# Row-by-row fetching by SP and ACT in the second layer's edge sweep, and PSUM operands on VectorE beside GpSimd's gathers, in a four-layer graph network

## The chip, the cores and the metric

The kernel runs on one core of one Trainium2 chip. The metric is the device time of one execution in microseconds (us); three executions of the kernel before are shown. Engine names: PE (TensorE), DVE (VectorE), ACT (ScalarE), POOL (GpSimd), SP (SyncE). PSUM is the accumulator memory with 8 banks of 2 KB in each of 128 partitions, SBUF the working memory.

## What is computed

A graph of 12,500 nodes and 200,000 edges, sorted by destination, goes through four layers. Each adds its output to the node state x; x is normalised before each.

```python
x = x + L0(h, ...)      # attention, 1 head, batch norm, relu
x = x + L1(h, ...)      # attention, 4 heads, with 13 edge features in the logit
x = x + L2(h, ...)      # sum of 128 edge attributes per node, then a 3-layer MLP
x = x + L3(h, ...)      # one weight matrix per edge type (8), mean over a node's edges
# attention, layers L0 and L1:
alpha = leaky_relu(a_src[src] + a_dst[dst] (+ a_edge))
out   = segment_sum(softmax_over_dst(alpha) * h[src], dst) + bias
# L3:
msg = einsum('nd,rdo->rno', x, W_rel)[edge_type, src]
out = relu(x @ W_self.T + b + segment_sum(msg, dst) / deg)
```

## The kernel before

**Layout.** Nodes are padded to 128 x 98 (partition p holds nodes 98p to 98p+97, in NK = 14 chunks of JB = 7 columns). Edges are padded to 128 x EC = 1568, and each partition's 1568 edges form GK = 8 strands of 196. A sweep over the edges takes NG = 98 groups of GC = 16 columns; a group is 2 steps of all 8 strands. Because the edges are sorted by destination, a sweep is a running sum along each strand that a factor 0 cuts where the destination changes; the table `keep` holds 1 or 0 per edge.

**Stages**, one after the other, all five engines meeting in `finish_stage` (L171) between them:

1. graph: edge borders, counts, node tables, the table of layer A (L0).
2. expansion and edge sweep of layer A (also sums the 128 edge attributes).
3. node stage A (`nodes_a_stage`): softmax division, batch norm, table of layer B.
4. expansion and edge sweep of layer B (L1).
5. node stage B (`nodes_b_stage`): L1's end, the MLP L2, the relation table for L3.
6. sweep over the relation table (`edges_rel_stage`, "rel").
7. last node stage (`nodes_rel_stage`).

**A sweep.** POOL issues one indirect DMA per column: 128 rows of the node table, one for each partition, picked by an index column in SBUF (`src` for layers A and B at L1077, `rel_row` for rel at L2036). A group's rows lie in one of NS = 6 slots (5 in layer A). POOL may start on group g when the store of group g-6 has landed and group g-5 is summed. DVE then makes the logits (L1213 to L1233), ACT the exponentials (L1134) and, in layer B, a copy of the edge terms (L1136); DVE multiplies the rows (L1246) and adds the running sums (L1190, L1195, two of each per group; one operand is in PSUM). SP stores the group (L1111, in rel L2052), 1120 KB in layer B.

**Help in the rel sweep.** For every second group from 7 to 95 (45 groups, the list `HELPED`) POOL issues 15 gathers rather than 16. The rows of the last column are fetched by plain one-row DMAs whose source row comes from a register: `fetch_rows` (L1988) loads 32 indices from `helped_row` into registers (L1991), then for each one fixes the address (L1993) and issues one DMA (L1994). SP does 32 rows after each group's store, ACT 32 rows after each group's L2069, so that two group times give the 128 rows. The table `helped_row` is `rel_row`'s columns turned by PE: it is made at the start of node stage B (DVE L1872, L1874, PE L1942, DVE L1878). PE's program there first waits for all seven weight loads of ACT's queue (L1763).

**Expansion** (`Expand`). The destination logits lie at the first edge of each node and are spread along the edges by a scan, one per head (L715), whose two inputs are `keep` and the logits, both in SBUF. In layer B the edge terms are then added to all heads (L755), and a scan per head sums the edge terms themselves (L759). POOL meanwhile gathers the first groups of the sweep.

**Node stages.** POOL gathers seven columns of the sums per chunk (L1280). In stage A `AttentionNodes.v_join` multiplies both parts by their factors (L1373, L1375) and adds them (L1377), 896 elements per partition each, all operands in SBUF; the next bias is added at L1512. The sums have two buffers: chunk k+2 is gathered once chunk k is joined. In the last stage each chunk takes three such operations (L2154, L2156, L2158), with three buffers.

## Time and profile before

| | us |
|---|---|
| runs | 7205.66, 7193.89, 7196.95 (median 7196.95) |
| profiled execution | 7196.47, of which span 7194.6 |
| POOL busy | 5087.8 (71% of the span), 5295 instructions |
| DVE busy | 3425.5 (48%) |
| ACT busy | 985.2 (14%) |
| PE busy | 624.0 (9%) |

A busy time counts an engine's own instructions; DMA issues and register loads on SP and ACT are not in it. POOL's time is that of the indirect DMAs it issues. A "mean ns" is the duration of one; POOL also spends some 300 ns between two of them, shown as idle time released by "issue".

### The profile page before, as it was taken

The numbers are of one execution on the slowest core, as the hardware profiler recorded it, in microseconds if no ns is written. First come the engines' busy times: TensorE is split into PE (matmuls) and PEld (weight loads), VectorE is DVE, ScalarE is ACT, GpSimd is POOL, SyncE is SP. The second block draws the span as 40 slices with busy tenths as digits, with TensorE's granted clock in tenths as the row PEclk, the third lists the DMA queues.
The fourth block names the chain that finished last, engine by engine and source line by source line (L and its number), as shares of the span: only waits on it lengthen the run. The fifth ranks groups of instructions, "written<-read, shape, count | busy, mean of one in ns | idle before, by whom it ended". The sixth has DMA issues, their size and how long they took to land. (4 is left out here: it accounts for less than half of the span.)

```text
span 7194.6 us, 39656 instructions
## 1 busy us (share of the span) xinstructions
PE 624.0 (9%) x2403; PEld 426.9 (6%) x2403; DVE 3425.5 (48%) x6202; ACT 985.2 (14%) x3082; POOL 5087.8 (71%) x5295
## 2 busy tenths in 40 slices
PE   1100000000001530000000000058411000000000
PEld 1100000000000420000000000024200000000000
DVE  8466666666666664444444444478322222222223
ACT  2122222222222120000000000056200000000000
POOL 5777777777775577777777777633477777777776
PEclk7555555555555665555555555579755555555555
DMA  5366767676765423333333333345333333333332
GB/s 182 111 213 210 224 210 225 209 226 209 225 209 180 147 98 113 115 115 115 115 115 115 115 115 115 101 160 201 139 107 108 113 108 107 110 110 107 107 112 86
DMA packets 334692, 1044.18 MB, mean 145 GB/s; under 512 B 106489, under 2 KB 128764, under 8 KB 296514
## 3 DMA queue, kind: packets, MB, share of 16 engines
q1 hardware_dynamic: 151986, 668.92, 25.9%
q0 software_dynamic: 173632, 368.42, 20.3%
q10 hardware_dynamic: 8784, 4.31, 0.2%
q14 instruction: 271, 2.22, 0.1%
q8 instruction: 19, 0.31, 0.0%
HBM read 527.27 MB, written 513.96 MB: 145 GB/s over the span
## 5 line engine op out<-in xcount | busy, mean ns | idle before, releaser
L1077 POOL DMA_INDIRECT edge_rows<-table_b,src_i x1568 | 1502.2, 958 | 477.8 <-issue 477.8
L1077 POOL DMA_INDIRECT edge_rows<-table_a,src_i x1568 | 1483.9, 946 | 477.9 <-issue 477.9
L2036 POOL DMA_INDIRECT edge_rows<-table_rel,rel_row x1523 | 1437.0, 944 | 510.3 <-issue 462.8
L2121 DVE TENSOR_TENSOR edge_rows<-edge_rows,ps 128x1024 f32<-128x1024 f32 x195 | 238.0, 1221 | 1386.9 <-DMA edge_rows<-table_rel,rel_row 1383.5
L1213 DVE TENSOR_TENSOR z<-edge_rows,dst_logit 128x16 f32<-128x16 f32 (+1 forms) x196 | 40.9, 209 | 1679.1 <-DMA edge_rows<-table_b,src_i 1026.4
L1195 DVE TENSOR_TENSOR edge_rows<-edge_rows,ps 128x1032 f32<-128x1032 f32 (+1 forms) x390 | 484.2, 1242 | 84.4 <-ACT edge_rows L1131 67.3
L1190 DVE TENSOR_TENSOR ps<-edge_rows,ps 128x1032 f32<-128x1032 f32 (+1 forms) x390 | 485.7, 1245 | 8.6 <-ACT edge_rows L1131 1.9
L1131 ACT ACTIVATE edge_rows<-edge_rows,weight_decay 128x129 f32<-128x129 f32 x1568 | 470.1, 389 | 0.0
L805 PE MATMUL ps<-ident,edge_rows 128*128 128x128 f32 x16 | 3.9, 426 | 3483.2 <-DVE edge_rows L1195 2034.1
L1134 ACT ACTIVATE ps<-weight_decay 128x128 f32<-128x128 f32 x98 | 27.5, 281 | 1893.4 <-DVE weight_decay L1233 1893.4
L2069 ACT ACTIVATE ps<-keep 128x16 f32<-128x16 f32 x98 | 19.6, 201 | 1850.7 <-DVE edge_rows L2121 1847.0
L2107 DVE TENSOR_TENSOR ps<-edge_rows,ps 128x1024 f32<-128x1024 f32 x195 | 239.5, 1228 | 35.9 <-DMA edge_rows<-table_rel,rel_row 29.2
L1246 DVE TENSOR_TENSOR edge_rows<-edge_rows,ps 128x2112 f32<-128x2112 f32 x98 | 230.7, 2354 | 35.3 <-ACT ps L1134 35.3
L1165 DVE TENSOR_TENSOR ps<-edge_rows,ps 128x1024 f32<-128x1024 f32 x195 | 239.5, 1228 | 0.0
L1173 DVE TENSOR_TENSOR edge_rows<-edge_rows,ps 128x1024 f32<-128x1024 f32 x195 | 236.7, 1214 | 0.1
L1127 ACT ACTIVATE weight_decay<-weight_decay 128x16 f32<-128x16 f32 x98 | 21.2, 216 | 1472.1 <-DVE weight_decay L1233 1472.1
L805 PEld LDWEIGHTS ps<-ident,edge_rows 128*128 128x128 f32 x16 | 3.1, 223 | 3483.8 <-issue 2034.4
L1934 PE MATMUL ps<-w_rel,own_part 128*128 128x512 f32 x392 | 196.7, 641 | 2.5 <-DVE rel L1838 1.2
L912 PE MATMUL ps<-ident,edge_rows 128*1 128x128 f32 (+1 forms) x16 | 3.8, 416 | 2037.5 <-DVE edge_rows L1195 2037.5
L1280 POOL DMA_INDIRECT node_sums<-sums_b,sum_row x98 | 102.5, 1046 | 93.5 <-DVE out_b L1377 52.1
L1751 POOL TENSOR_TENSOR x<-x,par 128x896 f32<-128x896 f32 x14 | 29.2, 2084 | 185.2 <-ACT hn L1645 185.2
L510 POOL DMA_INDIRECT piece<-dst_float,q_i x99 | 98.3, 993 | 79.3 <-DVE q_i L532 50.6
(284 smaller groups left out, 3211.9 us busy)
## 6 DMA issues: line engine op xcount, KB each, us to landing
sums_a<-edge_rows SPq DMA_DIRECT2D x98, 2064.0 KB, 8.2
sums_b<-edge_rows SPq DMA_DIRECT2D x98, 1120.0 KB, 4.7
edge_rows<-in_ea SPq DMA_DIRECT2D x98, 1024.0 KB, 11.8
sums_rel<-edge_rows SPq DMA_DIRECT2D x98, 1024.0 KB, 4.1
table_rel<-rel SPq DMA_DIRECT2D x98, 512.0 KB, 3.0
edge_rows<-table_rel ACTq DMA_DIRECT2D x2880, 0.5 KB
edge_rows<-table_rel SPq DMA_DIRECT2D x2880, 0.5 KB
edge_rows<-table_a,src_i POOLq DMA_INDIRECT x1568
```

Source lines behind the costliest of these rows:

```text
L1077: e.indirect_dma_start(out=rows[:, s, i, 0:L.W], out_offset=None, in_=L.table, in_offset=bass.IndirectOffsetOnAxis(ap=src[:, at:at + 1], a ...
L1131: done = e.activation(R[:, i, 0:NW], R[:, i, 0:NW], ACT.Copy, scale=wd[:, g % 2, 0, i, :])
L1165: attr_step.append(then(e.tensor_tensor(old_attr, before(g, t)[:, :, L.W:L.WS], bc(keep_now[:, t, :].unsqueeze(2), [P, GK, D]), ALU.mult)))
L1173: done = e.tensor_tensor(now, now, old_attr, ALU.add)
L1190: done = then(e.tensor_tensor(heads(old), heads(before(g, t)), bc(decay_now.unsqueeze(3), [P, GK, H, C + 1]), ALU.mult))
L1195: done = e.tensor_tensor(now, now, old, ALU.add)
L1246: t_weight = then(e.tensor_tensor(heads(R), heads(R), bc(factors[:, 0, :, :].unsqueeze(3), [P, GC, H, C + 1]), ALU.mult))
L1280: e.indirect_dma_start(out=self.buf[:, k % self.depth, b, :], out_offset=None, in_=self.sums, in_offset=bass.IndirectOffsetOnAxis(ap=sum_r ...
L1934: done = e.matmul(ps[:, 4 + 2 * (j % 2) + h, 0:half * D], own_part[:, j, :], w_rel[:, h * half:(h + 1) * half, :].rearrange("p r d -> p (r ...
L2036: e.indirect_dma_start(out=rows[:, s, i, :], out_offset=None, in_=table_rel, in_offset=bass.IndirectOffsetOnAxis(ap=rel_row[:, at:at + 1], ...
L2107: e.tensor_tensor(old, before, keep_now, ALU.mult).then_inc(step.sem, 1)
L2121: i = e.tensor_tensor(steps(g)[:, t, :, :], steps(g)[:, t, :, :], old, ALU.add)
```

## The change

It has three parts.

1. **Row-by-row fetching in layer B's sweep.** A class `Helped` takes the place of `fetch_rows` and serves both sweeps. In layer B (not in A) POOL drops the last column of the 45 groups 7, 9, ..., 95; SP and ACT fetch those rows, 140 elements each, in quarters of 32: SP quarter 0 of group g+4 and quarter 1 of g+3 after storing group g, ACT quarter 2 of g+3 and quarter 3 of g+2 after the exponentials and the copy of group g. Each of these calls waits first for the store of the group six before, and for the sum of the group five before, the one it is to fill. In the rel sweep the order stays as it was. Three semaphores take the place of four.
2. **The index tables** `helped_src` and `helped_rel` are both made in the graph stage (a memset, two copies, two transposes, two copies out of PSUM), and the four instructions at the start of node stage B go.
3. **PSUM operands.** ACT copies `keep` to PSUM (`near`) at the start of both expansions, and the scans read it there. In layer B the scan of a head writes to PSUM and the edge terms are added head by head, in place of one add over all heads. In node stage A the factors and the first product are in PSUM; in the last stage the inverse degrees and the mean are.

The core of the diff:

```diff
+    class Helped:
+        def fetch(self, e, regs, g, p0, n):
+
+            if g not in self.place:
+                return
+            h, s = self.place[g], g % self.NS
+            e.wait_ge(*self.stored[s].at(16 * (g // self.NS)))
+            e.wait_ge(*self.summed.at(g - self.NS + 2))
+            for p in range(p0, p0 + n, len(regs)):
+                m = min(len(regs), p0 + n - p)
+                e.load(regs[0:m], self.index[h:h + 1, p:p + m])
+                for i in range(m):
+                    row = e.snap(regs[i])
+                    e.dma_start(self.rows[p + i:p + i + 1, s, LAST, 0:self.W], self.table[bass.ds(row, 1), :]
+                                ).then_inc(self.fetched[h % 3].sem, 16)
...
-        def v_spread(self, e):
+        def s_near(self, e):
+            e.activation(self.near, keep[:, :], ACT.Copy).then_inc(self.keep_near.sem, 1)
+
+        def v_spread(self, e, terms=None):
...
             for h in range(self.L.H):
-                e.tensor_tensor_scan(self.dst_l[:, :, h], keep[:, :], self.dst_l[:, :, h], 0.0, ALU.mult, ALU.add
+                at = self.dst_l[:, :, h]
+                e.tensor_tensor_scan(at if terms is None else self.spread, self.near, at, 0.0, ALU.mult, ALU.add
                                      ).then_inc(step.sem, 1)
                 step.up()
+                e.wait_ge(*step.at(step.n))
+                if terms is not None:
+                    e.tensor_tensor(at, terms[:, :, h], self.spread, ALU.add).then_inc(step.sem, 1)
...
-                for i in range(GC):
+                for i in range(GC - (g in helped.place)):
...
+                if L.AE:
+                    helped.fetch(e, regs_sync, g + 4, 0, P // 4)
+                    helped.fetch(e, regs_sync, g + 3, P // 4, P // 4)
...
+                    helped.fetch(e, regs_scalar, g + 3, P // 2, P // 4)
+                    helped.fetch(e, regs_scalar, g + 2, 3 * P // 4, P // 4)
...
-            then(e.tensor_tensor(a[:, :, :, 0:C], a[:, :, :, 0:C], bc(of_sums.unsqueeze(3), wide), ALU.mult))
+            then(e.tensor_tensor(part, a[:, :, :, 0:C], bc(by_sums.unsqueeze(3), wide), ALU.mult))
...
-            t = then(e.tensor_tensor(b[:, :, :, 0:C], b[:, :, :, 0:C], bc(of_own.unsqueeze(3), wide), ALU.mult))
-            e.wait_ge(*step.at(t))
-            e.tensor_tensor(out, a[:, :, :, 0:C], b[:, :, :, 0:C], ALU.add).then_inc(self.joined.sem, 1)
+            t = then(e.tensor_tensor(b[:, :, :, 0:C], b[:, :, :, 0:C], bc(by_own.unsqueeze(3), wide), ALU.mult))
+            e.wait_ge(*step.at(t))
+            e.tensor_tensor(out, b[:, :, :, 0:C], part, ALU.add).then_inc(self.joined.sem, 1)
...
-            nodes.v_logit(e, 0, step)
-            e.wait_ge(*helped_turned.at(1))
-            then(e.tensor_copy(helped_row[:, :], ps[:, 1, 0:P]))
+            nodes.v_logit(e, 0, step)
...
-                t = then(e.tensor_tensor(r, r, bc(inv_deg[:, span(k)].unsqueeze(2), [P, JB, D]), ALU.mult))
+                if k >= 1:
+                    e.wait_ge(*out_ready.at(k))
+                t = then(e.tensor_tensor(mean, r, bc(inv_near[:, span(k)].unsqueeze(2), [P, JB, D]), ALU.mult))
                 e.wait_ge(*step.at(t))
-                t = then(e.tensor_tensor(r, r, chunk(own_part, k), ALU.add))
+                t = then(e.tensor_tensor(mean, chunk(own_part, k), mean, ALU.add))
                 e.wait_ge(*step.at(t))
-                e.scalar_tensor_tensor(r, r, 0.0, chunk(x, k), ALU.max, ALU.add).then_inc(out_ready.sem, 1)
+                e.scalar_tensor_tensor(r, mean, 0.0, chunk(x, k), ALU.max, ALU.add).then_inc(out_ready.sem, 1)
```

**What stands in a row on the engines.** ACT in layer B's sweep, with the change, at the first helped group (`weight_decay` are the log weights, `helped_src` the index table, `ISA` fixes an address in a register; the pair ISA and DMA stands 32 times):

```order
L1211 ACTIVATE ps<-weight_decay 128x128 [waits edges_for_exp]
L1213 ACTIVATE edge_rows<-edge_logit 128x16x4
L240 TENSOR_LOAD helped_src [waits edges_summed,edges_stored1]
L242 ISA
L243 DMA edge_rows<-table_b 1x140
L242 ISA
L243 DMA edge_rows<-table_b 1x140
```

Before, ACT's two activations of a group were followed at once by those of the next group; now a load and 32 row DMAs stand between them.

DVE in layer B's expansion, before (a scan is printed as SCALAR_TENSOR_TENSOR):

```order
L711 COPY dst_logit<-first_logit 128x4
L715 SCALAR_TENSOR_TENSOR dst_logit<-keep,dst_logit 128x1568 x4
L752 MEMSET keep 128x8
L755 TENSOR_TENSOR dst_logit<-dst_logit,edge_logit 128x6272
L759 SCALAR_TENSOR_TENSOR edge_logit<-keep,edge_logit 128x1568 x4
```

and with the change:

```order
L774 COPY dst_logit<-first_logit 128x4
L780 SCALAR_TENSOR_TENSOR ps<-ps,dst_logit 128x1568
L785 TENSOR_TENSOR dst_logit<-edge_logit,ps 128x1568
L780 SCALAR_TENSOR_TENSOR ps<-ps,dst_logit 128x1568
L785 TENSOR_TENSOR dst_logit<-edge_logit,ps 128x1568
L780 SCALAR_TENSOR_TENSOR ps<-ps,dst_logit 128x1568
L785 TENSOR_TENSOR dst_logit<-edge_logit,ps 128x1568
L780 SCALAR_TENSOR_TENSOR ps<-ps,dst_logit 128x1568
L785 TENSOR_TENSOR dst_logit<-edge_logit,ps 128x1568
L827 MEMSET keep 128x8
L827 MEMSET ps 128x8
L831 SCALAR_TENSOR_TENSOR edge_logit<-ps,edge_logit 128x1568 x4
```

Each of the large operations now has one input in PSUM and one in SBUF; the add is cut in four and stands between the scans.

DVE at the start of node stage B, before (L1325 to L1338 make the first chunk's logits, L1361 begins its join):

```order
L1872 MEMSET helped_f 128x128
L1874 CAST helped_f<-rel_row 128x45
L1325 TENSOR_TENSOR self_logit<-own_rows,node_logit_b 128x28
...
L1338 TENSOR_TENSOR self_ex<-self_logit,self_max 128x28
L1878 CAST helped_row<-ps 128x128
L1361 TENSOR_TENSOR den<-node_sums,self_ex 128x28
```

and with the change:

```order
L1406 TENSOR_TENSOR self_logit<-own_rows,node_logit_b 128x28
L1409 TENSOR_TENSOR self_max<-node_sums,inv_deg 128x28
...
L1418 TENSOR_TENSOR self_ex<-node_sums,self_max 128x28
L1419 TENSOR_TENSOR self_ex<-self_logit,self_max 128x28
L1450 TENSOR_TENSOR den<-node_sums,self_ex 128x28
```

The copy out of PSUM between the logits and the join is gone, and with it DVE's wait for PE there.

## Rows read from the trace of the kernel before

**Rows 1.** Groups of instructions by line, POOL alone: busy us, mean ns | idle us, releasers

```profile
L1077 POOL DMA_INDIRECT edge_rows<-table_b,src_i x1568 | 1502.2, 958 | 477.8 <-issue 477.8
L1077 POOL DMA_INDIRECT edge_rows<-table_a,src_i x1568 | 1483.9, 946 | 477.9 <-issue 477.9
L2036 POOL DMA_INDIRECT edge_rows<-table_rel,rel_row x1523 | 1437.0, 944 | 510.3 <-issue 462.8 <-SPq L171 45.7 <-DVE edge_rows L2121 1.8
L1280 POOL DMA_INDIRECT node_sums<-sums_a,sum_row x98 | 110.0, 1122 | 57.2 <-issue 28.3 <-SPq L171 17.6 <-DVE agg L1377 7.4
L1280 POOL DMA_INDIRECT node_sums<-sums_rel,sum_row x98 | 104.0, 1061 | 37.4 <-issue 29.6 <-POOLq L171 7.8
```

**Rows 2.** One line's instructions: duration ns min/median/max, first and last start us

```profile
L1077 POOL DMA_INDIRECT edge_rows<-table_b,src_i x1568: 940/944/6627, 2660.9 to 4639.7; - x196
L2036 POOL DMA_INDIRECT edge_rows<-table_rel,rel_row x1523: 940/944/963, 5122.9 to 7023.6; - x191
L1280 POOL DMA_INDIRECT node_sums<-sums_rel,sum_row x98: 940/944/1859, 7052.8 to 7185.4; - x98
```

**Rows 3.** Groups by line and form, DVE, both from layer B's sweep

```profile
L1190 DVE TENSOR_TENSOR ps<-edge_rows,ps 128x1056 f32<-128x1056 f32 x195 | 245.4, 1259 | 3.4
L1213 DVE TENSOR_TENSOR z<-edge_rows,dst_logit 128x64 f32<-128x64 f32 x98 | 22.2, 227 | 1026.4 <-DMA edge_rows<-table_b,src_i 1026.4
```

**Rows 4.** Timeline of layer B's expansion: start us, duration us, instruction

```profile
2669.95 13.38 DVE L715 TENSOR_TENSOR_SCAN dst_logit<-keep,dst_logit 128x1568 f32<-128x1568 f32 x4
...
2683.50 6.69 DVE L755 TENSOR_TENSOR dst_logit<-dst_logit,edge_logit 128x6272 f32<-128x6272 f32 x1
2684.38 6.63 POOL L1077 DMA_INDIRECT edge_rows<-table_b,src_i  x1 [0.30 <-issue]
2690.22 13.38 DVE L759 TENSOR_TENSOR_SCAN edge_logit<-keep,edge_logit 128x1568 f32<-128x1568 f32 x4
...
2704.65 0.94 POOL L1077 DMA_INDIRECT edge_rows<-table_b,src_i  x1 [0.30 <-issue]
```

**Rows 5.** Timeline of layer A's expansion

```profile
326.25 3.42 DVE L715 TENSOR_TENSOR_SCAN dst_logit<-keep,dst_logit 128x1568 f32<-128x1568 f32 x1
326.60 3.83 POOL L1077 DMA_INDIRECT edge_rows<-table_a,src_i  x1 [0.30 <-issue]
```

**Rows 6.** Timeline of the rel sweep, SP and ACT: one turn of 32 rows each

```profile
5887.31 0.40 SPq L2052 DMA_DIRECT2D sums_rel<-edge_rows  x1
5892.17 13.48 SPq L1994 DMA_DIRECT2D edge_rows<-table_rel  x32
...
5887.32 0.20 ACT L2069 ACTIVATE ps<-keep 128x16 f32<-128x16 f32 x1 [19.64 <-DVE edge_rows L2121]
5891.78 13.08 ACTq L1994 DMA_DIRECT2D edge_rows<-table_rel  x32
```

**Rows 7.** Timeline of layer B's sweep, ACT: one group's two activations

```profile
3405.58 0.28 ACT L1134 ACTIVATE ps<-weight_decay 128x128 f32<-128x128 f32 x1 [19.55 <-DVE weight_decay L1233]
3405.80 0.24 ACT L1136 ACTIVATE edge_rows<-edge_logit 128x64 f32<-128x64 f32 x1
```

**Rows 8.** Timeline of node stage A, POOL: three gathers in a row, one chunk

```profile
2477.46 1.21 POOL L1280 DMA_INDIRECT node_sums<-sums_a,sum_row  x1 [0.30 <-issue]
2478.97 1.54 POOL L1280 DMA_INDIRECT node_sums<-sums_a,sum_row  x1 [0.30 <-issue]
2480.81 1.82 POOL L1280 DMA_INDIRECT node_sums<-sums_a,sum_row  x1 [0.30 <-issue]
```

**Rows 9.** Timeline of the last node stage: the stretched gather of one chunk

```profile
7171.11 1.84 POOL L1280 DMA_INDIRECT node_sums<-sums_rel,sum_row  x1 [0.30 <-issue]
```

**Rows 10.** Timeline of the start of node stage B

```profile
4696.84 0.25 ACT L1343 ACTIVATE self_ex<-self_ex 128x56 f32<-128x56 f32 x1 [20.34 <-DVE self_ex L1338]
...
4700.47 0.29 DVE L1878 CAST helped_row<-ps 128x128 int32<-128x128 f32 x1 [3.65 <-PE ps L1942]
4700.67 0.19 DVE L1361 TENSOR_TENSOR den<-node_sums,self_ex 128x28 f32<-128x28 f32 x1
```

More of the change, by code:

```diff
@@ L202, in natural, with every, helped_columns, __init__ @@
         return i % GK * NC + g * GS + i // GK
-    HELP_EVERY = 2
-    HELPED = list(range(7, NG - 1, HELP_EVERY))
+    LAST = GC - 1
+    def every(n, first):
+        return {g: h for h, g in enumerate(range(first, NG - 1, n))}
+    def helped_columns(ap, place):
+        at = [natural(g, LAST) for g in place]
+        return ap[:, at[0]:at[-1] + 1:at[1] - at[0]]
+    helped_b = every(2, 7)
+    class Helped:
+        def __init__(self, name, place, index, table, W, rows, NS, stored, summed):
+            self.place, self.index, self.table, self.W = place, index, table, W
+            self.rows, self.NS, self.stored, self.summed = rows, NS, stored, summed
+            self.by_pool = {g: 16 * sum(GC - (i in place) for i in range(g % NS, g + 1, NS)) for g in range(NG)}
+            self.fetched = [sem(f"{name}_helped{i}") for i in range(3)] if place else []
+        def all_by_pool(self, slot):
+            return self.by_pool[max(g for g in range(NG) if g % self.NS == slot)]
+        def fetch(self, e, regs, g, p0, n):
[11 more added lines that the diff above has]
+                                ).then_inc(self.fetched[h % 3].sem, 16)
+        def wait(self, e, g):
+            if g in self.place:
+                h = self.place[g]
+                e.wait_ge(*self.fetched[h % 3].at(16 * P * (h // 3 + 1)))
     def sum_rows(sums, g):
@@ L683, in tensor @@
                     table.t_turn(e, i)
+            e.wait_ge(*helped_floated.at(2))
+            for i in range(2):
+                done = e.transpose(ps[:, 7, i * P:(i + 1) * P], helped_f[:, i, :], ident[:, :])
+            done.then_inc(helped_turned.sem, 1)
         return Programs(sync, scalar, gpsimd, vector, tensor)
@@ L1028, in attention_edges @@
         factors = ps[:, 7, 0:2 * GC * H].rearrange("p (i c h) -> p i c h", i=2, c=GC)
-        gathered = [sem_of(f"edges_gathered{i}", 16 * GC * turns(NG, NS, i)) for i in range(NS)]
         stored = [sem_of(f"edges_stored{i}", 16 * turns(NG, NS, i)) for i in range(NS)]
@@ L1033, in attention_edges @@
         summed = sem_of("edges_summed", NG)
+        helped = Helped(L.name, helped_b if L.AE else {}, helped_src, L.table, L.W, rows, NS, stored, summed)
+        gathered = [sem_of(f"edges_gathered{i}", helped.all_by_pool(i)) for i in range(NS)]
         def spare(i):
@@ L1358, in v_join @@
             of_sums, of_own = self.ex[:, s, 0, :, :], self.ex[:, s, 1, :, :]
+            if self.near is None:
+                by_sums, by_own, part = of_sums, of_own, a[:, :, :, 0:C]
+            else:
+                if k >= 1:
+                    e.wait_ge(*self.joined.at(k))
+                factors, part = self.near
+                by_sums, by_own = [factors[:, i * JB * H:(i + 1) * JB * H].rearrange("p (j h) -> p j h", h=H)
+                                   for i in range(2)]
             out = self.out_of(k).rearrange("p j (h c) -> p j h c", h=H)
@@ L1987, in nodes_b_stage @@
         return Programs(sync, scalar, gpsimd, vector, tensor)
-    def fetch_rows(e, regs, table, out, of, h, p0, n, fetched):
-        e.load(regs[0:n], helped_row[h:h + 1, p0:p0 + n])
-        for m in range(n):
-            row = e.snap(regs[m])
-            e.dma_start(out[p0 + m:p0 + m + 1, of, GC - 1, :], table[bass.ds(row, 1), :]).then_inc(fetched.sem, 16)
     def edges_rel_stage(local, own_part):
@@ L2019, in edges_rel_stage @@
         summed = sem_of("edges_summed", NG)
+        helped = Helped("rel", helped_b, helped_rel, table_rel, D, rows, NS, stored, summed)
+        gathered = [sem_of(f"edges_gathered{i}", helped.all_by_pool(i)) for i in range(NS)]
         crossing = Crossing("cross", rows[:, (NG - 1) % NS, GC - GK:GC, :], sb("border_state", [P, NV + 1])[:, :],
@@ L2033, in gpsimd @@
                     e.wait_ge(*summed.at(g - NS + 2))
-                for i in range(GC - (g in place)):
+                for i in range(GC - (g in helped.place)):
                     at = natural(g, i)
@@ L2199, in _ @@
         def _(e):
+            regs_sync.extend(e.alloc_register(f"row_sync{i}") for i in range(32))
             graph.sync(e)
@@ L2217, in _ @@
         def _(e):
+            regs_scalar.extend(e.alloc_register(f"row_scalar{i}") for i in range(32))
             graph.scalar(e)
```

103 lines of the change are left out of this document (54 added, 49 removed).

## The prediction

> **What bounds the kernel now.** I read three views, in this order. First the groups of instructions of POOL [rows 1]: the two attention sweeps are 1568 gathers each and the rel sweep 1523, every one about 945 ns busy with some 305 ns of "issue" behind it. In all three the idle time is issue and next to nothing else: POOL never waits for a free slot, so it sets the pace. Then one line's instructions with first and last start [rows 2]: in layer B 1568 gathers go from 2660.9 to 4639.7 us; in rel 1523 go from 5122.9 to 7023.6, a pitch of 1900.7 / 1522 = 1.249 us. Last DVE [rows 3]: in layer B it sat idle 1026 us for gathered rows, 10.5 us a group. What shortens POOL's row of gathers shortens these stages one for one; what DVE or ACT do there costs nothing until it exceeds a group's time of 16 x 1.249 = 20.0 us.
>
> **Why some gathers are long.** In layer B's expansion the timeline [rows 4] shows a gather of 6.63 us that starts during the add of 6.69 us (L755) and ends 0.8 us after it. Both inputs of that add are in SBUF. Under the scans, which also have both inputs there, the gathers take some 3.0 to 3.3 us: from 2660.9 [rows 2] to 2704.65 [rows 4] POOL starts 17 gathers, 43.8 us, where its own pitch would need far less. Layer A's one scan stretches one gather to 3.83 us [rows 5]. In the sweeps DVE runs operations of 1.26 us with one operand in PSUM, 195 of the shown form alone [rows 3], and POOL's median stays at 944 ns [rows 2]. So a long DVE operation with two SBUF inputs holds a gather back, and one with a PSUM operand does not. I take that as the mechanism.
>
> Against it stands the Trainium skill, page "SBUF — State Buffer", section "Who interferes with whom", which tells of a probe in which `tensor_tensor` did not stall a GpSimd DMA, and infers that descriptor generation does not need the interface that the second input takes. By that rule part 3 of the change would be worth nothing. The same section also has two SBUF inputs contend with a GpSimd instruction that reads SBUF; the gathers of this kernel take their indices from SBUF, and the 6.63 us row sides with this second statement.
>
> **The change, part by part.**
>
> *Layer B's sweep.* POOL issues 45 gathers less. Its pitch there after the expansion is (4639.7 - 2704.65) / 1550 = 1.2484 us [rows 2, 4], and 45 x 1.2484 = **56.2 us**. That is a gain only if SP and ACT keep up. A pair of groups now takes POOL 31 gathers, 38.7 us, 19.35 us a group; the shorter group takes 18.7. SP's turn in the rel sweep runs from 5887.31 to 5892.17 + 13.48 = 5905.65, 18.3 us, of which 4.5 us are the register load and the hops around it and 13.5 the 32 DMAs [rows 6]. ACT's turn there is 5887.32 to 5904.86, 17.5 us. In layer B ACT gives up an activation of 0.20 us and has two that end 0.46 us after their start [rows 7]: 17.8 us. So SP has 1.0 us to spare per group and ACT 1.5, and DVE, which now also waits for ACT's exponentials with a row turn queued ahead of them, has its 10 us. SP's store of a group now has a row turn of the group before ahead of it, as in rel already. The row is 560 bytes rather than 512. No row shows what that does to an issue; one bound is nothing, the other proportion to bytes, 9.4% of 13.5 us or 1.3 us, with which SP would take 19.6 us, 0.3 us over the pace, 91 x 0.3 = 27 us of loss. I take nothing, since a store of 1024 KB takes SP 0.40 us to issue, no more than a row of 512 bytes with its address work, 13.48 / 32 = 0.42 us [rows 6]: issuing does not go by bytes.
>
> *Layer B's expansion.* 17 gathers at their own pitch need 21.2 us in place of 43.8: **22.6 us**. All nine disturbed ones lie under operations that now have a PSUM input. DVE's own chain stays about as long (eight scans, the add in four parts) and ends near 2704; POOL has six slots, 120 us of gathers, so nothing waits for it. ACT's copy of `keep` runs while DVE waits for the logits. The bounds are 0 (a scan that reads PSUM still blocks) and 22.6.
>
> *Layer A's expansion.* One gather goes from 3.83 to 0.94 us [rows 5]: **2.9 us**. Bounds 0 and 2.9.
>
> *Node stage A.* The 98 gathers are 110.0 us busy at a mean of 1122 ns [rows 1]; at 944 ns they would take 92.5, so 17.5 us are stretch. Three gathers of a chunk show it [rows 8]: 1.21 under the bias add, which stays as it is, 1.54 and 1.82 under the three operations of the join, which change. Per chunk that is 0.6 + 0.9 = 1.5 us, some 20 us if all 14 chunks had it; the total allows 17.5 less 14 x 0.27 for the bias, 13.7. The sums have two buffers, and POOL already waited 7.4 us for joins [rows 1]; a faster POOL will wait more, a few times. I take **12 us**, with bounds of 4 and 20.
>
> *Last node stage.* POOL gathers back to back. 13 chunks have one gather like the 1.84 us one [rows 9]; busy time 104.0 less 98 x 0.944 leaves **11.4 us**. All three operations change, and there are three buffers, so nothing takes its place: each chunk is then 8.7 us of gathers against 3.3 us of DVE. Bounds 8 and 11.5.
>
> *Start of node stage B.* ACT's exponentials end at 4697.09; DVE begins the join at 4700.67, since it waits for PE's transpose, which is behind the weight loads [rows 10]. Without the copy it can begin at some 4697.2: **3.5 us**. The stage is a chain of DVE, ACT and PE that starts there. Bounds 0 (the matrices are needed a step later anyway) and 3.5.
>
> *Graph stage.* The new table work is a handful of operations like the 0.29 us copy [rows 10], below 2 us of DVE. I cost it at nothing; DVE there ends long before POOL's last scatter. If that cover were gone it would cost these 2 us.
>
> Sum: 56.2 + 22.6 + 2.9 + 12 + 11.4 + 3.5 = 108.6. The profiled execution is 7196.5, which gives 7087.9; the median of the runs is 0.5 above it, so **7088 us**, 1.5% faster. A measurement of this kernel tells about 0.2% (14 us) from no change.
>
> **Rivals.**
>
> *A: the PSUM operands free nothing.* By the page's first statement above the sum is 56.2 + 3.5 = 59.7, 7137 us. The rows against it are the 6.63 and 3.83 us gathers. For it: no row shows a scan with a PSUM input beside a gather. 4%.
>
> *B: the row turns do not fit.* SP or ACT is a little slower per row in layer B than in rel, and the sweep goes at their pace for 91 groups. At 19.6 us for SP (the bytes bound) the time is 7088 + 27 = 7115. For it speaks how little room there is, 1.0 us of 18.3; against it that rel runs with the same turns at its own pitch, DVE waiting for gathers alone. 8%.
>
> *C: slower than before.* The same mechanism taken further: ACT stands in every group's chain, since DVE cannot weight the rows before ACT's exponentials, and ACT now issues 32 DMAs between two of them. Should the DMA queue push back (the stores are 1120 KB, in rel 1024), ACT's turn grows. The sweep gains nothing from a turn of 20.0 us on, 69 ns a row more than in rel; to eat the other 52 us as well it takes 0.57 us more for each of 91 groups, a turn of 20.6, or 495 ns a row in place of 409 [rows 6]. At 21.5 us it would be 7196 + 91 x 1.5 - 52 = 7281. In rel nothing like it is seen. 5%, of which 2 stop near the point of balance.
>
> *D: node stage A gives all or more.* If POOL's waits there shrink with the stretch, 20 us rather than 12: 7080. 12%; and if new waits take it back, 4 rather than 12: 7096. 13%.
>
> **How the numbers follow.** The forecast as it stands 58%, A 4%, B 8%, C 5%, D 25% with both signs. The range takes the forecast, both sides of D and half of B: 7070 to 7108. Slower by over 0.2% is most of C, 0.03; within 0.2% the rest of C, 0.02; all else is faster, 0.95.
>
> **What the profile after would show.** Layer B's sweep has 1523 gathers, issue as the only idle time, and no gather above 1 us in the expansion though the scans run. SP's and ACT's turns are as long as in rel, and DVE waits for POOL's rows, not for the helped ones. In the last stage every gather is 0.94 us; in node stage A one of 1.2 to 1.5 us per chunk is left. DVE starts node stage B's first join right behind the exponentials. The forecast is wrong if DVE's wait in layer B is on one-row DMAs or on ACT, if POOL there shows a wait for DVE or a store, or if gathers stay stretched under a scan that reads PSUM.

## The result and the profile after

The changed kernel takes 7092.65 us (median of 7098.0, 7091.91, 7089.11 and 7093.38) against 7196.95 before: a ratio of 0.9854, 95% interval 0.9837 to 0.9871, so 1.5% faster. The profiled execution is the longest of the four, 7098.0 us with a span of 7095.8.

POOL's groups, busy us, mean ns | idle us with what ended it, answer to [rows 1]:

```profile
L1151 POOL DMA_INDIRECT edge_rows<-table_a,src_i x1568 | 1482.6, 946 | 477.8 <-issue 477.8
L1151 POOL DMA_INDIRECT edge_rows<-table_b,src_i x1523 | 1439.0, 945 | 464.5 <-issue 464.5
L2099 POOL DMA_INDIRECT edge_rows<-table_rel,rel_row x1523 | 1438.8, 945 | 509.9 <-issue 463.7 <-SPq L173 45.7 <-DVE edge_rows L2181 0.6
...
L1360 POOL DMA_INDIRECT node_sums<-sums_a,sum_row x98 | 96.5, 984 | 63.2 <-issue 27.4 <-SPq L173 19.2 <-DVE agg L1466 12.6
...
L1360 POOL DMA_INDIRECT node_sums<-sums_rel,sum_row x98 | 92.6, 945 | 37.4 <-issue 29.6 <-POOLq L173 7.8
```

In layer B's sweep POOL issues 45 gathers less, and its only idle time is still issue (its own time between two gathers): the row turns of SP and ACT fit (a turn is what SP or ACT does for one group: a register load and 32 one-row DMAs). DVE waits there 944.5 us for POOL's gathers and not once for a one-row DMA. The mean went from 958 to 945 ns, so the long gathers of the expansion are gone as well. The last stage is back at the plain duration. Node stage A kept 4 us of stretch (96.5 against 98 x 0.945) and waits 12.6 us for DVE's join in place of 7.4.

One line's instructions, with min/median/max and first and last start, answer to [rows 2]:

```profile
L1151 POOL DMA_INDIRECT edge_rows<-table_b,src_i x1523: 940/945/966, 2651.4 to 4553.6; - x191
```

The longest of the 1523 is 966 ns; before it was 6627. Taken from such first and last starts, the stages moved like this:

| POOL's gathers | before, us | after, us | difference | predicted |
|---|---|---|---|---|
| layer A's sweep | 1960.5 | 1959.2 | -1.3 | -2.9 |
| node stage A | 147.8 | 139.5 | -8.3 | -12 |
| layer B's sweep, expansion included | 1978.8 | 1902.2 | -76.6 | -78.8 |
| from node stage B's first gather to rel's | 440.6 | 437.6 | -3.0 | -3.5 |
| rel sweep | 1900.7 | 1902.0 | +1.3 | 0 |
| last node stage | 132.6 | 121.2 | -11.4 | -11.4 |

The rows add up to -99.3 and the gaps between them to +0.5: -98.8, which is the difference of the two spans, 7194.6 and 7095.8. The profiled execution after is the longest of its four, so the medians differ by more, 104.3.

The timeline of layer B's expansion (start us, duration us, instruction) answers to [rows 4]:

```profile
2680.05 3.43 DVE L780 TENSOR_TENSOR_SCAN ps<-ps,dst_logit 128x1568 f32<-128x1568 f32 x1
2680.19 0.94 POOL L1151 DMA_INDIRECT edge_rows<-table_b,src_i  x1 [0.30 <-issue]
...
2683.52 3.01 DVE L785 TENSOR_TENSOR dst_logit<-edge_logit,ps 128x1568 f32<-128x1568 f32 x1
2683.94 0.95 POOL L1151 DMA_INDIRECT edge_rows<-table_b,src_i  x1 [0.30 <-issue]
```

Gathers that start inside a scan or an add now take 0.94 and 0.95 us. SP's and ACT's turns in layer B's sweep answer to [rows 6, 7]:

```profile
3112.33 0.40 SPq L1185 DMA_DIRECT2D sums_b<-edge_rows  x1
3117.32 13.26 SPq L243 DMA_DIRECT2D edge_rows<-table_b  x32
3131.06 0.40 SPq L1185 DMA_DIRECT2D sums_b<-edge_rows  x1
```

```profile
3104.58 0.28 ACT L1211 ACTIVATE ps<-weight_decay 128x128 f32<-128x128 f32 x1 [19.66 <-DVE weight_decay L1313]
3104.80 0.24 ACT L1213 ACTIVATE edge_rows<-edge_logit 128x64 f32<-128x64 f32 x1
3106.96 14.08 ACTq L243 DMA_DIRECT2D edge_rows<-table_b  x32
```

SP's turn is 3130.58 - 3112.33 = 18.25 us and ACT's 3121.04 - 3104.58 = 16.5. ACT's rows are a little slower than in rel (440 ns in place of 409), but its register load takes 2.15 us there against 4.08.

### The profile page after: what moved, and what is told of

It is laid out like the page before. It is cut to its first block and busy times, and to the rows that moved or that the text cites. A ratio compares the mean times of both kernels' runs of the same rounds, so it can differ in the third digit from the quotient of the medians.

```text
span 7095.8 us, 57426 instructions
## 1 busy us (share of the span) xinstructions
PE 615.7 (9%) x2404; PEld 417.4 (6%) x2404; DVE 3430.4 (48%) x6209; ACT 988.0 (14%) x3084; POOL 5001.1 (70%) x5250
## 5 line engine op out<-in xcount | busy, mean ns | idle before, releaser
L1151 POOL DMA_INDIRECT edge_rows<-table_b,src_i x1523 | 1439.0, 945 | 464.5 <-issue 464.5
L1293 DVE TENSOR_TENSOR z<-edge_rows,dst_logit 128x16 f32<-128x16 f32 (+1 forms) x196 | 40.6, 207 | 1594.7 <-DMA edge_rows<-table_b,src_i 944.5
```

The lines of the kernel that those rows point to most:

```text
L1151: e.indirect_dma_start(out=rows[:, s, i, 0:L.W], out_offset=None, in_=L.table, in_offset=bass.IndirectOffsetOnAxis(ap=src[:, at:at + 1], a ...
```

## The experiments

Unless a text says otherwise, each changes the changed kernel, and the ratio is to the kernel before in the same session (a session is one set of executions on one chip). Where a text gives microseconds above the changed kernel, they are above its 7092.65, taken in a session in which the kernel before took 7196.95; in the two sessions of the first eight experiments it took 7198.46 and 7198.08, so such a difference is good to some 3 us.

**The row turns alone undone.**

```diff
-        helped = Helped(L.name, helped_b if L.AE else {}, helped_src, L.table, L.W, rows, NS, stored, summed)
+        helped = Helped(L.name, {}, helped_src, L.table, L.W, rows, NS, stored, summed)
```

> The changed kernel without SP's and ACT's row turns in layer B's sweep; POOL gathers all 1568 there again, all PSUM operands stay. Theory (POOL's row of gathers is the whole gain of the turns): 45 x 1.2498 = 56 us longer than the changed kernel, all of it in layer B's sweep, which then takes 1902 + 56 = 1958 us; total 7149, against 7093 with the turns and 7197 before. Rival (the turns cost something beside the gain, in ACT's place in the chain or in the queue of stores): the difference is below 50 us, and the other stages change too.

Measured: 7148.9 us, ratio 0.9932 (0.9915 to 0.9948), 56.3 us above the changed kernel. The groups have 1568 gathers of layer B at the plain mean:

```profile
L1151 POOL DMA_INDIRECT edge_rows<-table_b,src_i x1568 | 1479.7, 944 | 477.8 <-issue 477.8
```

Its gathers start over 1956.2 us, where other runs with 1523 of them at 944 ns take 1900.6: 55.6 us, against 56.2 predicted. No other stage moved by more than the spread of the gathers' own pitch. The turns cost nothing where they stand.

**The PSUM operands alone undone.** Scans, adds, join and last stage as before; both sweeps keep their turns.

```diff
-                e.tensor_tensor_scan(at if terms is None else self.spread, self.near, at, 0.0, ALU.mult, ALU.add
+                e.tensor_tensor_scan(at if terms is None else self.spread, keep[:, :], at, 0.0, ALU.mult, ALU.add
...
-                t = then(e.tensor_tensor(mean, r, bc(inv_near[:, span(k)].unsqueeze(2), [P, JB, D]), ALU.mult))
+                t = then(e.tensor_tensor(r, r, bc(inv_deg[:, span(k)].unsqueeze(2), [P, JB, D]), ALU.mult))
```

> The changed kernel with the row turns in both sweeps but without the PSUM operands: the spreading of logits in both layers, the join of node stage A and the last node stage read and write SBUF as before. Theory (a DVE operation with two SBUF inputs holds a gather back, one with a PSUM input does not): longer than the changed kernel by 20.4 (layer B's expansion) + 2.9 (layer A's) + 8.3 (node stage A) + 11.4 (last stage) = 43 us, total 7136; the four stages get their times of before back. Rival (these stages became shorter because of the turns or by chance): no difference, 7093.

Measured: 7137.15 us, ratio 0.9913 (0.9897 to 0.993), 44.5 above the changed kernel, 43 expected. By first and last gather: layer B 1923.9 us, node stage A 146.8, last stage 131.6. The parts of the change add up: 56.3 + 44.5, and 3.0 for the start of node stage B, which neither run undoes, are 103.8 against the 104.3 between the medians of before and after. By the ratios the two are 56.1 and 42.5, together with the 3.0 101.6: the parts add up within some 3 us, and the closer match is luck.

**One half of layer B's expansion undone.** The first four scans read `keep` from PSUM but write SBUF; the add and the last four scans have two SBUF inputs.

```diff
-            expand.v_spread(e, edge_logit)
+            expand.v_spread(e)
...
+            e.tensor_tensor(dst_l[:, :, :], dst_l[:, :, :], edge_logit[:, :, :], ALU.add).then_inc(step.sem, 1)
...
-                e.tensor_tensor_scan(edge_logit[:, :, h], expand.near, edge_logit[:, :, h], 0.0, ALU.mult, ALU.add
+                e.tensor_tensor_scan(edge_logit[:, :, h], keep[:, :], edge_logit[:, :, h], 0.0, ALU.mult, ALU.add
```

> The changed kernel, only layer B's expansion altered: the four scans that spread the logits still read keep from PSUM (but write SBUF), while the add is one operation with two SBUF inputs again and the four scans of the edge terms read keep from SBUF. Theory (it goes operation by operation): the gathers beside the first four scans stay at 0.95 us; one beside the add is some 6.6 us, four beside the last scans some 3.1 us each, together 5.7 + 4 x 2.2 = 14 us of stretch; total 7107. Rival (it is the sum of the traffic, or where the result is written, that counts): the gathers beside the first scans are long as well, which write SBUF again, and the total is 7113.

Measured: 7108.48 us, ratio 0.9874 (0.9857 to 0.989), 15.8 above the changed kernel. Its timeline tells the operations apart:

```profile
2659.14 13.80 DVE L780 TENSOR_TENSOR_SCAN dst_logit<-ps,dst_logit 128x1568 f32<-128x1568 f32 x4
2660.09 0.94 POOL L1154 DMA_INDIRECT edge_rows<-table_b,src_i  x1 [0.31 <-issue]
...
2673.18 6.69 DVE L830 TENSOR_TENSOR dst_logit<-dst_logit,edge_logit 128x6272 f32<-128x6272 f32 x1
2673.82 6.87 POOL L1154 DMA_INDIRECT edge_rows<-table_b,src_i  x1 [0.30 <-issue]
2679.91 13.38 DVE L834 TENSOR_TENSOR_SCAN edge_logit<-keep,edge_logit 128x1568 f32<-128x1568 f32 x4
2680.99 3.09 POOL L1154 DMA_INDIRECT edge_rows<-table_b,src_i  x1 [0.31 <-issue]
```

All eleven gathers beside the first scans took 0.94 or 0.95 us although the scans write SBUF; one beside the add took 6.87 and four beside the last scans 3.0 to 3.1. In the profile before, the first four scans stood in the same place and took 13.38 us in place of 13.80 [rows 4]. Four gathers beside them took 3.0 to 3.3, the first of them

```profile
2670.88 3.25 POOL L1077 DMA_INDIRECT edge_rows<-table_b,src_i  x1 [0.30 <-issue]
```

The same operation holds a gather or doesn't, by one input.

**Does a result in PSUM do the same?** Two runs in the last stage, each with one operation that has both inputs in SBUF and writes PSUM. First the first operation of a chunk:

```diff
-                t = then(e.tensor_tensor(mean, r, bc(inv_near[:, span(k)].unsqueeze(2), [P, JB, D]), ALU.mult))
+                t = then(e.tensor_tensor(mean, r, bc(inv_deg[:, span(k)].unsqueeze(2), [P, JB, D]), ALU.mult))
```

> The changed kernel, in the last node stage only the first operation of each chunk altered: it reads the inverse degrees from SBUF again, so both its inputs are in SBUF, and writes its result to PSUM as before. Theory (what holds a gather is two inputs in SBUF): one gather of most chunks is stretched by up to that operation's 1.1 us; the 98 gathers take 3 to 9 us more than 92.6 and the stage 124 to 130 in place of 121.2; total 7095 to 7101. Rival (a result in PSUM is enough to keep the gathers free): 121.2 and 7092.

Measured: the stage took 121.1 us, all gathers 940 to 947 ns. That reads like the rival, but it isn't evidence: in 13 of the 14 chunks a gather had started up to 0.27 us ahead of that operation or within 0.02 us of its start, and the next one came behind its end or in its last 0.12 us. None started in its midst, so none could be held. The profile before agrees, in the same stage: gathers that started up to 0.03 us behind an operation weren't held, those at 0.05 to 0.10 took 1.81 to 1.86 us. (The run's total, 9763 us, belongs to a session of which more below.) So the second operation was altered instead, the one which a gather follows by 0.1 us:

```diff
-                t = then(e.tensor_tensor(mean, r, bc(inv_near[:, span(k)].unsqueeze(2), [P, JB, D]), ALU.mult))
+                t = then(e.tensor_tensor(r, r, bc(inv_near[:, span(k)].unsqueeze(2), [P, JB, D]), ALU.mult))
...
-                t = then(e.tensor_tensor(mean, chunk(own_part, k), mean, ALU.add))
+                t = then(e.tensor_tensor(mean, chunk(own_part, k), r, ALU.add))
```

> The changed kernel, in the last node stage the second operation of each chunk altered: it reads own_part and the sums, both in SBUF, and writes PSUM; the first reads its factors from PSUM and writes SBUF, the third has one PSUM input. The run that altered the first operation could not tell: no gather started between its begin and its end. The second operation is the one that a gather starts some 0.1 us behind, before the change and after. Theory (two inputs in SBUF hold a gather, wherever the result goes): that gather takes 1.82 us in about 11 of 14 chunks, the stage 11 x 0.88 = 10 us more than 121.2. Rival (the result in PSUM is enough): all gathers stay at 0.94 to 0.95 us and the stage at 121.2. Read from the stage, since the difference is near what the totals can tell.

Measured: 7115.68 us, ratio 0.9871 (0.9854 to 0.9887); the stage took 130.8 us, 9.6 more than 121.2. One chunk in its timeline:

```profile
7004.34 1.09 DVE L2220 TENSOR_TENSOR node_sums<-node_sums,ps 128x896 f32<-128x896 f32 x1 [6.17 <-DMA node_sums<-sums_rel,sum_row]
7004.41 0.94 POOL L1360 DMA_INDIRECT node_sums<-sums_rel,sum_row  x1 [0.30 <-issue]
7005.46 1.10 DVE L2222 TENSOR_TENSOR ps<-own_part,node_sums 128x896 f32<-128x896 f32 x1
7005.65 1.72 POOL L1360 DMA_INDIRECT node_sums<-sums_rel,sum_row  x1 [0.30 <-issue]
```

The gather behind L2220 (a PSUM input, result to SBUF) takes 0.94 us, the one behind L2222 (two SBUF inputs, result to PSUM) 1.72. Twelve chunks have such a gather of 1.72 to 1.80, and the five that start 0.05 to 0.07 us behind L2220 all take 0.94. It is the inputs, not where the result goes.

The Trainium skill, page "SBUF — State Buffer", section "Who interferes with whom", says that a DVE instruction with two SBUF inputs contends with a GpSimd instruction that reads SBUF, by an exclusive lock that goes to whoever is first. This run agrees on the inputs, with 1.72 against 0.94 us. Order matters here too: a gather that starts first keeps its 0.94 us, and DVE's operation behind it took 1.10 to 1.15 us in place of 1.09, so it is hardly delayed. The same section's report that `tensor_tensor` did not stall a GpSimd DMA is not borne out here: the gather beside the add of 6.69 us took 6.87. Which part of a gather is held, the read of its indices or another, no run shows.

**How near is SP's turn to the bound?** First the register load in two halves, in both of SP's fetches of layer B:

```diff
-                    helped.fetch(e, regs_sync, g + 4, 0, P // 4)
+                    helped.fetch(e, regs_sync[0:16], g + 4, 0, P // 4)
```

> The changed kernel with the 32 row numbers of each turn of SP in layer B loaded in two register loads of 16 with 16 rows behind each, in place of one load of 32; ACT is as it was. Theory (SP's turn of 18.25 us stands 1.1 us under POOL's pace of 19.35 us a group): a load of 16 takes between half the 4.1 us of one of 32 (then nothing changes, 7093) and as long as it. I take 3.3 us, a turn of 20.7, 1.35 us over the pace for 91 groups, +123 us, total 7216, slower than before; DVE's wait for gathered rows is then on SP's one-row transfers, and POOL waits for free slots. Rival (the turns are issued far enough ahead for a longer one to be hidden): no change, 7093, whatever the load takes.

Measured: 7096.01 us, ratio 0.9857 (0.9841 to 0.9874). My figure of 7216 was missed by 120 us; only the lower bound that I had named, no change, came out. The second load took 1.27 us where I had taken 3.3, and the turn became, in SP's timeline,

```profile
3110.22 0.40 SPq L1185 DMA_DIRECT2D sums_b<-edge_rows  x1
3114.20 14.95 SPq L243 DMA_DIRECT2D edge_rows<-table_b  x32
3129.24 0.40 SPq L1185 DMA_DIRECT2D sums_b<-edge_rows  x1
```

3129.24 - 3110.22 = 19.0 us, with no gap before the store. That is still under the pace of 19.35, so this run can't tell the theory from its rival. Then 36 rows for SP and 28 for ACT:

```diff
-                    helped.fetch(e, regs_sync, g + 4, 0, P // 4)
-                    helped.fetch(e, regs_sync, g + 3, P // 4, P // 4)
+                    helped.fetch(e, regs_sync[0:18], g + 4, 0, 36)
+                    helped.fetch(e, regs_sync[0:18], g + 3, 36, 36)
...
-                    helped.fetch(e, regs_scalar, g + 3, P // 2, P // 4)
-                    helped.fetch(e, regs_scalar, g + 2, 3 * P // 4, P // 4)
+                    helped.fetch(e, regs_scalar, g + 3, 72, 28)
+                    helped.fetch(e, regs_scalar, g + 2, 100, 28)
```

> The changed kernel with the rows of layer B's turns split 36 to SP and 28 to ACT, SP's in two loads of 18 rows each. The run with two loads of 16 left the time alone and showed SP's turn filled to 19.0 us, from one store to the next, with a second load of 1.3 us. Theory (POOL's pace of 19.35 us a group is the bound, and the queue of SP's turns can't be longer than that): four rows and four registers more are some 1.9 us, the turn 20.9, 1.55 us over the pace for 91 groups, +141 us, total 7234, slower than before; DVE waits for SP's one-row transfers and POOL for free slots. Rival (the slots hide a longer turn): 7093. In between lies a turn that packs tighter when nothing waits: 19.9 us would give +50.

Measured: 7445.55 us, ratio 1.0345 (1.0328 to 1.0363), 353 us over the changed kernel. The direction is the theory's, the size 2.5 times mine: both loads of 18 took 3.93 us, not one of them 1.3, and the turn became 23.8 us:

```profile
3332.92 0.40 SPq L1185 DMA_DIRECT2D sums_b<-edge_rows  x1
3337.24 19.36 SPq L243 DMA_DIRECT2D edge_rows<-table_b  x36
3356.70 0.40 SPq L1185 DMA_DIRECT2D sums_b<-edge_rows  x1
```

POOL now waits 333.1 us for stores of layer B, and DVE 1014 us for one-row transfers. From one store to the next it is 23.84 us on average, 4.5 over the pace, and 90 such turns would cost 404 us; 353 were measured, since the slots hide the first of them. A turn of 19.0 us costs nothing and one of 23.8 nearly all of its excess; the pace of 19.35 lies between.

**Node stage A: the bias in PSUM.** The first chunk's mean goes the same way.

```diff
+        bias_near, mean_near = ps[:, 7, D:2 * D], ps[:, 7, 2 * D:3 * D]
...
+            then(e.tensor_copy(bias_near, bn_par[:, 0, :]))
...
-                    done = e.tensor_tensor(chunk(agg, k), chunk(agg, k), over_nodes(bn_par[:, 0, :]), ALU.add)
+                    done = e.tensor_tensor(chunk(agg, k), chunk(agg, k), over_nodes(bias_near), ALU.add)
```

> The changed kernel, and in node stage A the bias, and the mean of the first chunk, are kept in PSUM, so that the bias add of each chunk has no second SBUF input. Theory: the last stretched gathers go, the 98 take 98 x 0.945 = 92.6 us in place of 96.5; the stage is up to 4 us shorter than 139.5, total 7089 to 7093, too little to tell by the total; by the stage it can be told. Rival (POOL's waits for a free buffer take all of it): those waits grow from 12.6 by the same 4 us and the stage stays at 139.5.

Measured: 7092.89 us, ratio 0.9855 (0.9838 to 0.9871); the stage 137.8 us, 1.7 less. Its group of gathers:

```profile
L1360 POOL DMA_INDIRECT node_sums<-sums_a,sum_row x98 | 92.6, 945 | 63.8 <-issue 27.1 <-DVE agg L1466 19.0 <-SPq L173 17.7
```

All stretch is gone (96.5 to 92.6), and waits took most of it. The wait for the join rose by more than that, from 12.6 to 19.0, but the changed kernel also had one wait of 3.9 us for PE, which is now among those for the join: together 16.5 before, 19.0 now.

**The same with three buffers of sums.** The third lies in the table's `rows`, unused in this part of the stage.

```diff
-            if k >= 2:
-                e.wait_ge(*self.joined.at(k - 1))
+            if k >= self.sums.depth:
+                e.wait_ge(*self.joined.at(k - self.sums.depth + 1))
...
-                if k >= 2:
-                    e.wait_ge(*turn_a.at(k - 1))
+                if k >= 3:
+                    e.wait_ge(*turn_a.at(k - 2))
```

> The kernel with the bias in PSUM, and node stage A's rows of sums in three buffers in place of two; the third is room that the stage's table uses only later. Theory (what POOL loses there to waits comes from having two buffers, while the rows of a chunk need some microseconds to land): the 12.6 us of waits for DVE's join go, the gathers run at 98 x 1.25 = 122.5 us plus little, total 7076 to 7080. Rival (DVE's chain for a chunk sets the stage's pace): POOL waits as long for the join before last, 7089 to 7093.

Measured: 7073.94 us, ratio 0.9829 (0.9813 to 0.9846). POOL's waits for the join are 0.9 and 0.3 us, its gathers take 121.2 us from first to last, 16.6 less than with two buffers. Nothing else was altered against the run before but what the third buffer needs. The gathers now stand in two groups:

```profile
L1364 POOL DMA_INDIRECT node_sums<-sums_a,sum_row x70 | 66.2, 945 | 38.9 <-issue 20.1 <-SPq L173 17.9 <-DVE agg L1470 0.9
L1364 POOL DMA_INDIRECT rows<-sums_a,sum_row x28 | 26.5, 945 | 8.5 <-issue 8.2 <-DVE agg L1470 0.3
```

**Row turns in layer A's sweep too.** On the changed kernel, every third group; ACT's turns behind its weighting:

```diff
+                else:
+                    helped.fetch(e, regs_sync, g + 4, 0, 28)
+                    helped.fetch(e, regs_sync, g + 3, 28, 28)
+                    helped.fetch(e, regs_sync, g + 2, 56, 28)
...
+                else:
+                    helped.fetch(e, regs_scalar, g + 3, 84, 22)
+                    helped.fetch(e, regs_scalar, g + 2, 106, 22)
```

> The changed kernel, and SP and ACT fetch the last gather's rows of every third group in layer A's sweep too: 31 groups from the 8th on, SP 28 rows in each of three turns, ACT 22 in each of two. POOL's pace there falls from 20.0 to 19.58 us a group. Theory (POOL's row of gathers is the only bound there too): 31 x 1.2498 = 39 us shorter, total 7054. Rival (the DMA engines are the next bound: their share in that sweep is 0.70, in layer B's 0.41; or ACT, which weights 16 columns a group between the turns, comes late): DVE waits for one-row transfers or for ACT, and the sweep takes the same time or longer, 7093 and more.

Measured: 7219.66 us, ratio 1.0029 (1.0018 to 1.0039), 127 us over the changed kernel; the sweep took 2066.7 us with 30 gathers less (I had counted 31). DVE and ACT in one group:

```profile
1345.26 0.18 DVE L1305 TENSOR_TENSOR z<-edge_rows,dst_logit 128x16 f32<-128x16 f32 x1
1356.33 1.23 DVE L1256 TENSOR_TENSOR ps<-edge_rows,ps 128x1024 f32<-128x1024 f32 x1 [10.89 <-issue]
```

```profile
1347.28 8.71 ACTq L246 DMA_DIRECT2D edge_rows<-table_a  x22
1356.04 0.20 ACT L1210 ACTIVATE ps<-keep 128x16 f32<-128x16 f32 x1 [14.56 <-issue]
```

DVE's group of that operation, in this run and in the last one of this section:

```profile
L1256 DVE TENSOR_TENSOR ps<-edge_rows,ps 128x1024 f32<-128x1024 f32 x195 | 239.6, 1229 | 469.7 <-issue 443.3 <-ACT ps L1210 26.3
```

```profile
L1255 DVE TENSOR_TENSOR ps<-edge_rows,ps 128x1024 f32<-128x1024 f32 x195 | 239.3, 1227 | 0.3 <-issue 0.3
```

DVE has the group's rows at 1345.3 and needs ACT's copy of `keep`, which is queued behind 22 rows until 1356.0. The view puts most of the wait down to issue, but ACT's copy, which starts 0.3 us ahead of the operation's start, is what ends it. But SP was late too. From one store to the next:

```profile
1314.45 0.40 SPq L1190 DMA_DIRECT2D sums_a<-edge_rows  x1
1321.56 11.90 SPq L246 DMA_DIRECT2D edge_rows<-table_a  x28
1333.56 0.56 SPq L1170 DMA_DIRECT2D edge_rows<-in_ea  x1
1334.16 1.87 SPq L1174 DMA_DIRECT2D feats<-in_ea  x1
1336.13 0.40 SPq L1190 DMA_DIRECT2D sums_a<-edge_rows  x1
```

That is 21.7 us without a gap, since the register load ahead of the rows takes up to 7.2 us in this sweep and two loads of inputs stand behind them. POOL needs only 19.58 us a group. SP's stores came 21.8 us apart on average, and DVE waited 237.7 us for one-row transfers. So the turns were too long on both queues. The rival was right in that the sweep became longer; how the 127 us divide between ACT's place and SP's length isn't shown, nor is a part of the DMA engines excluded.

So lighter turns behind that copy, every fourth group, on the kernel with three buffers:

```diff
                     e.activation(keep_now, group_columns(keep[:, :], g), ACT.Copy).then_inc(keep_copied.sem, 1)
+                    helped.fetch(e, regs_scalar, g + 2, 74, 27)
+                    helped.fetch(e, regs_scalar, g + 1, 101, 27)
```

> The kernel with three buffers of sums and the bias in PSUM (7074 us), and row turns in layer A's sweep, lighter and better placed than in the run that lost 127 us there: every fourth group (24), SP 28, 26 and 20 rows in three turns of four, ACT 27 rows in two, issued right behind the copy of keep and so no longer ahead of it. Pace of POOL 19.68 us a group. SP's register load took 4.1 to 7.2 us there and its turn 21.7; here its turns should be some 22, 21 and 19 us and the fourth 5, a mean of 17; ACT's turn some 20 in two of four groups. Theory (the loss was in the turns' length and in the copy of keep that waited behind them): 24 x 1.2498 = 30 us shorter, total 7044. Rival (with the stores and loads of this sweep any row turn of ACT ends ahead of none of DVE's needs): ACT's exponentials come late in two groups of four, DVE waits for them, and the total is 7074 to 7150.

This ran in a session in which the kernel before took 8852 us (10469.89 us, ratio 1.1836) and told nothing of its question. Again, in another session:

> The kernel of the run with row turns for every fourth group of layer A, unchanged, since in that session the kernel before itself took 8852 us in place of 7197 and row turns of every kernel were stretched. Theory as there: 7074 - 30 = 7044 us where the kernel before takes 7197. Rival: ACT's row turns come late for its exponentials, 7074 or more.

Measured: 7060.24 us, ratio 0.9791 (0.9775 to 0.9808), where the kernel before took 7209. It is the best version of this study, 2.1% faster than the kernel before, the changed kernel 1.5%. By the ratios the turns in layer A are worth 0.0038 x 7197 = 27 us, against 23 gathers x 1.25 = 29 (23 groups, where I had counted 24). DVE's wait ahead of the operation that reads the copy fell from 469.7 to 0.3 us. SP's turns were lightened in the same step (its stores are now 19.8 us apart on average), so this run does not part the two causes either.

## Why the prediction was right, step by step

The forecast was 7088 us; 7092.65 came out, within the range. The gain was 104.3 us where the terms add up to 108.6, and 98.5 between the two profiled executions. Most terms came out smaller than forecast, and node stage A's is the one that counts.

- *Layer B's sweep, 56.2 us*: shown alone as 56.3 us by the total and 55.6 by the stage.
- *The turns fit, SP with 1.0 us to spare*: shown from both sides, by a turn of 19.0 us for nothing and one of 23.8 for 353 us. That issuing does not go by bytes held for SP: 13.26 us for 32 rows of 560 bytes, 13.48 for 512. On ACT, where I had kept rel's figure, the rows took 14.08 in place of 13.08 and the load 2.15 in place of 4.08: a turn of 16.5 where I had 17.8, by two differences that no row had shown. Rivals B and C fall. Rival C's mechanism is real, though: in layer A's sweep ACT's turn stood ahead of an operation that DVE needs, and DVE waited 469.7 us there. The 127 us of that run are not its price alone, since SP's turn was over the pace as well.
- *Layer B's expansion, 22.6 us, and the mechanism*: confirmed operation by operation, and rival A falls with it. The size is less sharp: the stage table has 76.6 - 56.2 = 20.4, and the run with the PSUM operands undone took 1923.9 - 1902.2 = 21.7 longer there.
- *Last stage, 11.4 us*: 11.4. *Start of node stage B, 3.5 us*: 3.0 by the stage table; DVE now waits only 0.32 us, for the exponentials, ahead of its join. No run undid this part alone.
- *Node stage A, 12 us*: 8.3. This is the term that was mis-sized. I had put 13.7 of the 17.5 us of stretch to the join, less new waits. The busy time fell by 13.5 us, nearly as said, and 5.2 of it went to waits for the join (7.4 to 12.6), where I had left 1.7 for them. With three buffers those waits are 1.2 us, so they belong to the number of buffers.
- *Layer A's expansion, 2.9 us*: the gather beside the scan went from 3.83 to 0.95 us, as said. The whole stage fell by only 1.3, since its other gathers were some 1 ns longer, 1.5 us over 1568 of them. One of 2.12 us, 2.37 before, stayed beside the product of the edge weights, which still has two SBUF inputs.
- The profiled execution also has gathers 1 ns longer than the one before (945 for 944), which is some 5 us over 4600 gathers and was in no term. The runs of the study have means from 944 to 947 for the same instruction, also within one session (944 in the run with the second operation altered, 946 in the one beside it). So the nanosecond can't be put down to the change; what sets it is open.

## What to carry to other kernels

A DVE operation with two SBUF inputs holds back an indirect DMA of GpSimd that starts beside it (0.94 us became 6.87 beside an add of 6.69); one input in PSUM frees it, a result in PSUM does not. When freeing them shortens a stage less than the stretch, look at the buffers next: the wait has moved there. Work handed to an idle queue is free only up to the bound's pace and only behind the operations that others wait for; measure its turn from one fixed instruction to the next. And measure in more than one session: a turn with 1.1 us to spare became the bound in one of them (see below).

## What the runs showed of the hardware that I had not expected

**A session in which the issuing queues were slow.** In one session the kernel before took 8852 us, the changed one with a single operand of the last stage altered 9763, ratio 1.1034 (1.101 to 1.1057), and the one with turns in layer A as well 10470. In the profile of the second the gathers (944 ns) and DVE's adds were as long as ever. What differed is when SP and ACT got on. ACT in layer A's sweep, where there is no row turn at all:

```profile
505.53 3.72 ACT L1208 ACTIVATE edge_rows<-edge_rows,weight_decay 128x129 f32<-128x129 f32 x12
510.25 0.40 ACT L1208 ACTIVATE edge_rows<-edge_rows,weight_decay 128x129 f32<-128x129 f32 x1 [1.00 <-issue]
511.65 0.40 ACT L1208 ACTIVATE edge_rows<-edge_rows,weight_decay 128x129 f32<-128x129 f32 x1 [1.00 <-issue]
```

and SP's rows in layer B's sweep, 29.06 us where they had taken 13.26:

```profile
3522.79 0.40 SPq L1185 DMA_DIRECT2D sums_b<-edge_rows  x1
3527.54 29.06 SPq L243 DMA_DIRECT2D edge_rows<-table_b  x32
3556.70 0.40 SPq L1185 DMA_DIRECT2D sums_b<-edge_rows  x1
```

The instructions of a queue came in bursts, with steps of 0.7 and 1.4 us between them. A turn of 32 rows is some 130 instructions in a straight line (a DMA, a move and two register operations a row), and it pays for each burst. That the instructions were fetched more slowly would be a guess; no run tests it, and why it was so in that session stays open. What is measured is the price: there the turn shown is 33.9 us, SP's stores in layer B's sweep come 32.6 us apart on average, both sweeps take their time from it (3077.8 and 2987.6 us for 1902 each), and a kernel that differs from the changed one by one operand is 10% slower than the kernel before. In the session that timed the changed kernel it was 1.5% faster, and in three others runs that differ from it by one detail were 1.3 to 1.5% faster.

**Register loads.** One load of 32 registers from SBUF took 4.1 to 4.6 us on SP and 2.1 to 2.2 on ACT in layer B, about 4 on both in rel. In layer A, where SP loads 20 to 28, it took up to 9.6. A second load of 16 right behind the first took 1.27, one of 18 took 3.93. What decides it stays open.

**Adds of one head.** The four adds of 1568 elements with stride 4 take 2.90 to 3.01 us each, 12 together, where one add of 6272 took 6.69 [rows 4]. DVE had the time here. Neither stride nor PSUM was tried alone.
